# Weights of a mixture of experts on one core: each 1 MB load issued as two of 512 KB

## The chip, the core and the metric

The kernel runs on one core of one Trainium2 chip. The metric is the device time of one execution in microseconds. All arithmetic is float32.

## The reference, cut to what matters

Eight batches (`b`) of 100 tokens with 512 features go through a gated attention-like product with a context of 722 rows per batch, and then through a feed-forward layer with 16 experts, of which each token uses one.

```python
def reference(x, ctx_1024, router_w, w1, b1, w2, b2):
    # xn = layernorm(x)
    x1 = xn @ ctx_1024.T                      # per batch: 100 x 722
    h  = gelu_tanh(x1) * x1
    x  = x + h @ ctx_1024                     # 100 x 512
    # t = layernorm(x), all 800 tokens
    logits = t @ router_w                     # 800 x 16
    assign = argmax(logits)
    g   = sigmoid(logits[assign])
    hh  = gelu(t @ w1[assign] + b1[assign])   # w1: 16 x 512 x 1024
    out = hh @ w2[assign] + b2[assign]        # w2: 16 x 1024 x 512
    return x + g * out
```

Each expert has 2 MB of `w1` and 2 MB of `w2`, so the 16 experts have 64 MB of weights, and all of them are read once.

## The kernel before, in words

The program is written for each engine by hand, with semaphores between them. It has two stages.

**Attention, for b in 0 to 7.** SyncE (SP) loads the transposed context in two parts (`ctxT_a`, `ctxT_b`, line 271), the context itself (lines 266 to 268) and `x` (line 262). Buffers for two batches alternate, so each load for batch b + 2 waits until the products of batch b are done. TensorE computes `x1` (L399) and the second product (L406), VectorE (DVE) the layernorm, the product with the gelu, the residual and the routing: the expert of a token and its rank among that expert's tokens. GpSimd (POOL) scatters each batch's tokens, sorted by expert, into the DRAM tensor `rows` with an indirect DMA (L946).

**Experts.** The sorted tokens are handled in units of 32 tokens of one expert. An expert with more than 32 tokens has several units, and the first expert's first unit and those of the next three (the head) start before the last batch is routed. Per unit j TensorE transposes the tokens (L489), runs `first_layer` (L469, 16 products that the trace shows as x32) and then `second_layer` (L481, 32 products, x64) of unit j - 1. DVE transposes and adds the bias (L804, L810), ScalarE (ACT) does the gelu (L598), DVE the gate and the residual (L828), and POOL scatters the result to the output (L996). Unit lists are computed on the chip: POOL and SP read them from small tables (`colof`, L255) to fetch the units' rows (`load_extra`, L256), and SP fetches the first unit of every expert with `load_first` (L321).

**Weights.** The buffers hold expert 0 (`W1x`, `W2x`) and four slots; slot s takes experts s + 1, s + 5, s + 9 and s + 13. Each of an expert's two matrices is loaded as two halves of 1 MB. `load_half` (L273) issues one half as one DMA from SP (L276): for each of 128 partitions one contiguous piece of 2048 floats, 8 KB, and 16 is added to the half's own semaphore when it has landed. `first_layer` waits for the first half's semaphore before k = 0 and for the second's before k = 2; `second_layer` waits the same way before c = 0 and c = 4. A slot is filled once per round g, so the value waited for is 16 g + 16.

**Order of SP's queue.** What SP issues is carried out in its order, and its waits hold up all that is behind them. During attention, `EARLY` says how many halves are issued after the transposed context of batch b: 0, 0, 1, 1, 1, 2, 4, 3 for b = 0 to 7. Then SP issues two halves (into `W2x`), waits for the scattered rows, issues `load_first`, two halves, two `load_extra`, eight more of `load_first`, the rest of `b2` (L345), and four halves. The halves thus issued fill expert 0's buffers and the four slots. The rest is `next_weights` (L359): when the last unit that needs a slot's `w1` is done (`s_hp`), SP issues the next expert's two halves of `w1`; when it is done with `w2` (`s_y`), the two of `w2`.

```python
def load_half(half, slot, src, signals, h):
    dst = half(slot, h)
    n = dst.shape[1]
    sp.dma_start(dst, src[:, n * h:n * h + n]).then_inc(signals[h], 16)
```

Of the kernel before, what the change touches and what calls it, by code (L numbers as in the profile page):

```python
# [18 lines left out]
E, F = 16, 1024  # L19
# [18 lines left out]
SLOTS = 4  # L38
# [11 lines left out]
EPS = 1e-5  # L50

EARLY = (0, 0, 1, 1, 1, 2, 4, 3)

C_ID, C_NH = 0, P
# [47 lines left out]
def build(nc, x, ctx_main, ctx_rest, ctxT_a, ctxT_b, router, w1, b1, w2, b2, consts, out):  # L103
# [3 lines left out]
    with ExitStack() as stack:  # L107
# [79 lines left out]
        def second_half(slot, h):  # L187
            n = KF // 2
            if slot is None:
                return W2x[:, n * h:n * h + n, :]  # L190
            if slot == SLOTS - 1:
                return late[h][:, :].rearrange("p (k d) -> p k d", k=n)
            return W2[:, slot, n * h:n * h + n, :]
# [56 lines left out]
        def units(eng):  # L250
            return eng.value_load(ends[0:1, E - 1:E], min_val=SLOTS + E, max_val=MAXU)
# [8 lines left out]
        def _(sp):  # L260
# [9 lines left out]
            def load_ctxT(b, part):  # L270
                sp.dma_start(ctxTs[b % 2][part], (ctxT_a, ctxT_b)[part][b]).then_inc(s_ctxT[b % 2][part], 16)

            def load_half(half, slot, src, signals, h):  # L273
                dst = half(slot, h)
                n = dst.shape[1]
                sp.dma_start(dst, src[:, n * h:n * h + n]).then_inc(signals[h], 16)  # L276

            def both(half, slot, w, signals):
                return [(half, slot, w, signals, 0), (half, slot, w, signals, 1)]
# [11 lines left out]
            def load_weights(n):  # L291
                for _ in range(n):
                    load_half(*next(early_weights))
# [11 lines left out]
            for b in range(NB):  # L305
                if b + 2 < NB:
                    for part in range(2):
                        sp.wait_ge(s_x1ps[part], b + 1)
                        load_ctxT(b + 2, part)
                load_weights(EARLY[b])  # L310
                if b + 2 < NB:
# [47 lines left out]
            def next_weights(s, before, first, second):  # L359
                sp.wait_ge(s_hp, before)  # L360
                load_half(first_half, s, first, s_w1[s], 0)
                load_half(first_half, s, first, s_w1[s], 1)
                sp.wait_ge(s_y, before + 1)
                load_half(second_half, s, second, s_w2[s], 0)
                load_half(second_half, s, second, s_w2[s], 1)
# [15 lines left out]
        def _(pe):  # L381
# [5 lines left out]
            def transpose_x2(b):  # L387
                pe.wait_ge(s_x2, b + 1)
                for q in range(Q):
                    last = nc.tensor.transpose(p_t[:, T * q:T * q + T], row[:, b % RB, XW * q:XW * q + DQ],  # L390
                                               ident[0:T, 0:T])
                last.then_inc(s_tps, 1)
# [68 lines left out]
            def first_layer(j, slot, loaded):  # L461
                W, signals = (W1x, s_w1x) if slot is None else (W1[:, slot], s_w1[slot])
                pe.wait_ge(s_cur, j + 1)
                for k in range(KD):
                    if loaded is not None and k % 2 == 0:
                        pe.wait_ge(signals[k // 2], loaded)
                    for q in range(Q):
                        mine = W[:, k, :].rearrange("p (c q i) -> p c q i", c=KF, q=Q)[:, :, q, :]
                        last = nc.tensor.matmul(p_h[U * q:U * q + U, 0:FQ], curT[:, U * k:U * k + U], mine,  # L469
                                                start=(k == 0), stop=(k == KD - 1), tile_position=(0, U * q))  # L470
                last.then_inc(s_hp, 1)

            def second_layer(j, slot, loaded):
                signals = s_w2x if slot is None else s_w2[slot]
                pe.wait_ge(s_yo, j + 2)
                pe.wait_ge(s_act, j + 2)
                for c in range(KF):
                    if c % (KF // 2) == 0:
                        pe.wait_ge(signals[c // (KF // 2)], loaded)
                    for q in range(Q):  # L480
                        last = nc.tensor.matmul(p_y[U * q:U * q + U, 0:DQ], hT[:, U * c:U * c + U],  # L481
                                                second_half(slot, c // (KF // 2))[:, c % (KF // 2), DQ * q:DQ * q + DQ],
                                                start=(c == 0), stop=(c == KF - 1), tile_position=(0, U * q))
                last.then_inc(s_y, 1)

            def transpose_tokens(j):
                pe.wait_ge(s_next, j + 1)
                pe.sem_inc(s_apart_t, 1)
                nc.tensor.transpose(p_blk[:, 0:P], cur, ident).then_inc(s_blk, 1)  # L489
# [1 line left out]
            pe.sem_inc(s_y, 1)  # L491
            transpose_tokens(0)
            transpose_x2(NB - 1)
            first_layer(0, None, 16)
            transpose_tokens(1)
            logits(NB - 1)
            pe.wait_ge(s_b2, 16)
# [3 lines left out]
            ranks(NB - 1)  # L501
            nc.tensor.matmul(p_lg[:, 0:E], ones, hot_sum[:, :], start=True, stop=False)
            nc.tensor.matmul(p_lg[:, 0:E], ones, hot[:, :], start=False, stop=True).then_inc(s_cntps, 1)
            first_layer(1, 0, 16)
            transpose_tokens(2)
            second_layer(0, None, 16)
            pe.wait_ge(s_tab, 16)
            pe.wait_ge(s_pos, NB)
            nc.tensor.matmul(p_rk[0:1, 0:MAXU], unit_f[:, 0:1], ident[0:MAXU, 0:MAXU], start=True, stop=False)
            nc.tensor.matmul(p_rk[0:1, 0:MAXU], unit_f[:, 1:2], packing, start=False, stop=True)  # L510
            nc.tensor.matmul(p_rk[0:1, 64:64 + EXTRA], unit_f[:, 2:3], picked[:, :], start=True, stop=True
                             ).then_inc(s_eofps, 1)
            first_layer(2, 1, 16)
            transpose_tokens(3)
            second_layer(1, 0, 16)
            first_layer(3, 2, 16)
            second_layer(2, 1, 16)
            transpose_tokens(4)
            def end_of(e, least):
                at = slice(e, e + 1) if isinstance(e, int) else bass.ds(e, 1)  # L520
                return pe.value_load(ends[0:1, at], min_val=SLOTS + least + 1, max_val=MAXU)

            def further(first, end, slot, loaded):
                with pe.If(end > first + 1):
                    with pe.Fori(first + 1, end) as j:
                        first_layer(j, slot, None)
                        transpose_tokens(j + 1)
                        second_layer(j - 1, slot, loaded)

            def change(first, slot, loaded, prior, was):
                first_layer(first, slot, loaded)
                transpose_tokens(first + 1)
                second_layer(first - 1, prior, was)

            pe.wait_ge(s_plan, 1)
            change(SLOTS, None, 16, SLOTS - 2, 16)
            end = end_of(0, 0)
            further(SLOTS, end, None, 16)  # L540
            change(end, 0, 16, None, 16)
            with pe.Fori(0, E // SLOTS) as g:
                loaded = pe.snap(16 * g + 16)
                first = end_of(SLOTS * g, 0)
                for s in range(SLOTS - 2):
                    end = end_of(SLOTS * g + (s + 1), s + 1)
                    further(first, end, s, loaded)
                    change(end, s + 1, loaded, s, loaded)
                    first = end
                end = end_of(SLOTS * g + (SLOTS - 1), SLOTS - 1)  # L550
                further(first, end, SLOTS - 2, loaded)

                with pe.If(g < E // SLOTS - 1):
                    first, end = end, end_of(SLOTS * g + SLOTS, SLOTS)
                    change(first, SLOTS - 1, loaded, SLOTS - 2, loaded)
                    further(first, end, SLOTS - 1, loaded)
                    change(end, 0, pe.snap(loaded + 16), SLOTS - 1, loaded)
            second_layer(units(pe) - 1, SLOTS - 2, 16 * (E // SLOTS))

        @block.scalar  # L560
        def _(act):
# [47 lines left out]
        def _(dve):  # L609
# [263 lines left out]
            hidden_bias(3, slice(3, 4))  # L873
            dve.wait_ge(s_eof, 2)
            e4, _, _, after4 = unit_of(SLOTS)
            e5, before5, mine5, after5 = unit_of(SLOTS + 1)
            dve.wait_ge(s_extra[0], 16)
# [184 lines left out]
```

## Time and profile before

| | |
|---|---|
| Median of 3 runs | 298.41 us (295.26 to 300.35) |
| The profiled execution | 296.02 us |
| Its span, first to last instruction | 294.4 us |
| Mean granted TensorE clock | 0.943 |
| PE busy | 243.8 us (83% of the span) |
| DVE, POOL, ACT busy | 120.8, 73.1, 32.4 us |
| SP's queue (q1): packets, MB, share of 16 engines | 18600, 94.48 MB, 86.4% |
| HBM read and written | 95.93 and 5.14 MB, 343 GB/s over the span |
| Half loads into the slots (`W<-in_w`), median from issue to landing | 17.9 us for 1024 KB |

PE is TensorE's matmuls, PEld its weight loads, which overlap them. SPq is the queue of SP's instructions. A DMA's packets are its contiguous pieces, and one small packet per DMA engine that signals completion. A share of 16 engines is the sum of the packets' durations, divided by 16 times the length of the stretch. The chain that ended last is followed back from the last instruction, at each step to what released it. "Issue" stands for time in which an engine waited for nothing that the profile shows.

### The profile page before, as it was taken

The page shows a single profiled execution, that of the slowest core. Times are in us where ns is not written, and L with a number is a line of the kernel's source. Part 1 is how long each engine was busy: PE and PEld are TensorE (multiplying, and loading weights), DVE is VectorE, ACT ScalarE, POOL GpSimd, SP SyncE. Part 2 cuts the span into 40 slices and gives each one's busy share as a digit, 9 for nine tenths or more (in the row PEclk, how much of TensorE's full clock was granted, in tenths as well). Part 3 has the DMA queues.
Part 4 walks back from the last instruction along what each step waited for, and adds up shares of the span by engine and source line. Part 5 has one row for each costly group of instructions (what it writes and reads, how often), then busy time and mean ns, then how long its engine had stood idle before and what let it go on. Part 6 is the DMA issues. An engine that isn't in the chain of part 4 may idle for free.

```text
span 294.4 us, 9782 instructions
## 1 busy us (share of the span) xinstructions
PE 243.8 (83%) x3767; PEld 171.6 (58%) x3768; DVE 120.8 (41%) x424; ACT 32.4 (11%) x76; POOL 73.1 (25%) x97
## 2 busy tenths in 40 slices
PE   0899999999999999995928399777997999679950
PEld 0769587686776845573515167545675666365740
DVE  3035344363443457544413045523544544354520
ACT  0411111110111102010000001101001101001100
POOL 2302032031224314455610111211221221212120
PEclk9999999999999997798877789979999999999995
DMA  6999799999999999799999995899999999999900
GB/s 243 382 383 366 262 337 374 353 365 383 353 414 382 343 378 416 272 323 180 160 325 416 416 380 216 317 340 420 426 419 423 421 424 422 422 421 420 391 28 8
DMA packets 22255, 100.98 MB, mean 343 GB/s; under 512 B 3978, under 2 KB 7950, under 8 KB 13016
## 3 DMA queue, kind: packets, MB, share of 16 engines
q1 hardware_dynamic: 18600, 94.48, 86.4%
q0 software_dynamic: 3488, 5.90, 6.4%
q8 instruction: 17, 0.28, 0.4%
q10 hardware_dynamic: 144, 0.27, 0.2%
q14 instruction: 6, 0.05, 0.0%
HBM read 95.93 MB, written 5.14 MB: 343 GB/s over the span
## 4 chain that ended last, share of the span: by engine, by line
PE 68%; DMA 15%; issue 9%; DVE 2%; SPq 2%; POOL 1%; DVEq 0%; POOLq 0%
PE bank L469 16%; PE bank L481 16%; PE bank L399 15%; PE bank L406 14%; DMA W<-in_w 9%; DMA area<-rows 3%; PE bank L489 2%; DMA rows<-area,pad_at 2%; PE bank L414 2%; PE bank L384 1%; PE bank L390 1%; DMA xs<-in_x 1%; SPq L276 1%; SPq L321 1%; PE bank L422 0%
## 5 line engine op out<-in xcount | busy, mean ns | idle before, releaser
L469 PE MATMUL bank<-W,area 128*32 128x256 f32 x928 | 63.2, 411 | 25.5 <-issue 22.7
L996 POOL DMA_INDIRECT out<-area,out_at x32 | 31.7, 990 | 116.4 <-DVE area L828 107.2
L469 PEld LDWEIGHTS bank<-W,area 128*32 128x32 f32 x928 | 31.0, 117 | 48.0 <-issue 31.7
L481 PE MATMUL bank<-W,area 128*32 128x128 f32 x1600 | 50.6, 279 | 1.8 <-DVE area L828 1.8
L399 PEld LDWEIGHTS bank<-late,area 128*128 128x128 f32 (+1 forms) x384 | 45.1, 195 | 4.7 <-issue 4.6
L481 PEld LDWEIGHTS bank<-W,area 128*32 128x32 f32 x1600 | 43.6, 112 | 5.6 <-DVE area L828 2.2
L406 PE MATMUL bank<-area,late 128*100 128x512 f32 (+1 forms) x96 | 46.8, 601 | 0.0
L399 PE MATMUL bank<-late,area 128*128 128x100 f32 (+1 forms) x384 | 45.5, 281 | 1.3 <-issue 1.3
L804 DVE STREAM_TRANSPOSE area<-bank 128x256 f32<-128x256 f32 x32 | 14.4, 450 | 65.5 <-PE bank L469 64.8
L598 ACT ACTIVATE area<-area 128x256 f32<-128x256 f32 x32 | 13.3, 416 | 153.2 <-PE bank L481 149.2
L946 POOL DMA_INDIRECT rows<-late,pos x8 | 8.6, 1074 | 49.5 <-DVE pos L676 41.4
L406 PEld LDWEIGHTS bank<-area,late 128*100 128x100 f32 (+1 forms) x96 | 13.7, 167 | 10.0 <-issue 10.0
L489 PEld LDWEIGHTS bank<-con,area 128*128 128x128 f32 x33 | 4.7, 143 | 18.5 <-issue 18.5
L632 DVE TENSOR_TENSOR late<-late,bank 128x300 f32<-128x300 f32 x16 | 7.4, 463 | 19.5 <-ACT late L570 19.5
L828 DVE SCALAR_TENSOR_TENSOR area<-bank,area 128x128 f32 (+1 forms) x28 | 9.8, 351 | 10.9 <-PE bank L481 5.6
L489 PE MATMUL bank<-con,area 128*128 128x128 f32 x33 | 11.2, 340 | 3.4 <-DVE area L794 3.3
L810 DVE TENSOR_TENSOR area<-area,b1s 128x256 f32<-128x256 f32 x32 | 13.5, 423 | 1.1 <-DVE area L804 0.2
L570 ACT ACTIVATE late<-bank 128x300 f32<-128x300 f32 x16 | 6.7, 421 | 56.8 <-PE bank L399 56.8
L794 DVE TENSOR_SCALAR area<-area 128x128 f32 (+1 forms) x28 | 10.1, 359 | 6.2 <-DMA area<-rows 4.7
L934 POOL TENSOR_TENSOR late<-ve_t,con 100x4 f32<-100x4 f32 x8 | 8.4, 1053 | 9.6 <-DVE ve_t L618 9.6
L564 ACT COPY late<-bank 128x400 f32<-128x400 f32 x16 | 7.9, 493 | 25.3 <-PE bank L384 21.3
L815 DVE SCALAR_TENSOR_TENSOR area<-xs,area (+1 forms) x28 | 9.8, 351 | 1.3 <-issue 0.4
(114 smaller groups left out, 180.8 us busy)
## 6 DMA issues: line engine op xcount, KB each, us to landing
W<-in_w SPq DMA_DIRECT2D x54, 1024.0 KB, 17.9
area<-in_ctx_main SPq DMA_DIRECT2D x8, 1280.0 KB
area<-in_ctxT_a SPq DMA_DIRECT2D x8, 768.0 KB, 8.9
late<-in_w SPq DMA_DIRECT2D x6, 1024.0 KB, 17.6
area<-in_ctxT_b SPq DMA_DIRECT2D x8, 676.0 KB, 8.0
W1x<-in_w SPq DMA_DIRECT2D x2, 1024.0 KB, 9.9
area<-in_w SPq DMA_DIRECT2D x2, 1024.0 KB, 23.6
xs<-in_x SPq DMA_DIRECT2D x8, 200.0 KB
```

Of the source, the lines that this page charges most:

```text
L399: last = nc.tensor.matmul((p_xa, p_xb)[part][0:n, T * c:T * c + T], ctxTs[b % 2][part][:, k, P * c:P * c + n], xnT[:, k, :], start=(k == 0 ...
L406: last = nc.tensor.matmul(p_att[0:T, :], hidT[0:CW[c], c, :], cxs[b % 2][0:CW[c], c, :], start=(c == 0), stop=(c == SC - 1))
L469: last = nc.tensor.matmul(p_h[U * q:U * q + U, 0:FQ], curT[:, U * k:U * k + U], mine, start=(k == 0), stop=(k == KD - 1), tile_position=(0 ...
L481: last = nc.tensor.matmul(p_y[U * q:U * q + U, 0:DQ], hT[:, U * c:U * c + U], second_half(slot, c // (KF // 2))[:, c % (KF // 2), DQ * q:D ...
L489: nc.tensor.transpose(p_blk[:, 0:P], cur, ident).then_inc(s_blk, 1)
L598: nc.scalar.activation(hT, h_pre, ACT.Gelu).then_inc(s_act, 1)
L794: nc.vector.tensor_scalar(cur, mine[:, 0:DQ], mine[:, DQ + 1:DQ + 2], mine[:, DQ + 2:DQ + 3], ALU.subtract, ALU.mult).then_inc(s_next, 1)
L804: nc.vector.transpose(h_pre, p_h[:, 0:FQ]).then_inc(s_hT, 1)
L810: nc.vector.tensor_tensor(view, view, bias.unsqueeze(3).to_broadcast([P, 2, Q, U]), ALU.add).then_inc(s_hb, 1)
L815: nc.vector.scalar_tensor_tensor(out=mine[:, 0:DQ], in0=bias, scalar=mine[:, DQ:DQ + 1], in1=mine[:, 0:DQ], op0=ALU.mult, op1=ALU.add).the ...
L828: nc.vector.scalar_tensor_tensor(out=y_out[:, at, :].rearrange("p o d -> p (o d)"), in0=p_y[:, 0:DQ], scalar=mine[:, DQ:DQ + 1], in1=mine[ ...
L996: nc.gpsimd.indirect_dma_start(out_q, bass.IndirectOffsetOnAxis(ap=out_at[:, r:r + 1], axis=0), y_out[:, r, :], None, bounds_check=last_ou ...
```

## The change

`load_half` issues two DMAs in place of one. Each has half of the columns: one contiguous piece of 1024 floats, 4 KB, in each of 128 partitions, 512 KB in all. Both add 16 to the half's semaphore, so the half is there at 32, and every wait for a half goes to multiples of 32 (`HALF`). No other operation changes, and buffers, slots and the order of the halves stay.

```diff
+HALF = 32
...
             def load_half(half, slot, src, signals, h):
                 dst = half(slot, h)
                 n = dst.shape[1]
-                sp.dma_start(dst, src[:, n * h:n * h + n]).then_inc(signals[h], 16)
+                for i in range(2):
+                    lo = n // 2 * i
+                    sp.dma_start(dst[:, lo:lo + n // 2], src[:, n * h + lo:n * h + lo + n // 2]
+                                 ).then_inc(signals[h], HALF // 2)
...
-            first_layer(0, None, 16)
+            first_layer(0, None, HALF)
...
             with pe.Fori(0, E // SLOTS) as g:
-                loaded = pe.snap(16 * g + 16)
+                loaded = pe.snap(HALF * g + HALF)
...
-            second_layer(units(pe) - 1, SLOTS - 2, 16 * (E // SLOTS))
+            second_layer(units(pe) - 1, SLOTS - 2, HALF * (E // SLOTS))
```

SP's queue between the attention and the expert stage, before the change; `W<-in_w` is a half of weights into a slot, `area<-in_w` one into `W2x`, `area<-rows` are token rows:

```order
L276 DMA W<-in_w 128x2048 x7
L276 DMA area<-in_w 128x2048 x2
L321 DMA area<-rows 32x4x132 x4
L276 DMA W<-in_w 128x2048 x2
L255 TENSOR_LOAD colof
L255 ISA x2
L256 ISA
L256 DMA area<-rows 128x1x132
```

The same place after it (the lines of code are three or four further down):

```order
L279 DMA W<-in_w 128x1024 x14
L279 DMA area<-in_w 128x1024 x4
L325 DMA area<-rows 32x4x132 x4
L279 DMA W<-in_w 128x1024 x4
L256 TENSOR_LOAD colof
L256 ISA x2
L257 ISA
L257 DMA area<-rows 128x1x132
```

Nothing changed places. Two more DMAs of half the size stand ahead of the read of `colof` and the first `load_extra`.

SP's queue in the loop over experts, one `next_weights`, before:

```order
L371 TENSOR_LOAD ends
L371 ISA x2
L276 ISA
L276 DMA W<-in_w 128x2048
L276 ISA
L276 DMA W<-in_w 128x2048
L363 REGISTER_ALU
L276 DMA W<-in_w 128x2048 x2
```

And after:

```order
L375 ISA x2
L279 ISA
L279 DMA W<-in_w 128x1024
L279 ISA
L279 DMA W<-in_w 128x1024
L279 ISA
L279 DMA W<-in_w 128x1024
L279 ISA
L279 DMA W<-in_w 128x1024
L367 REGISTER_ALU
L279 DMA W<-in_w 128x1024 x4
```

An expert's weights take eight DMAs in place of four, in the same order and behind the same two waits.

## Rows read from the trace of the kernel before

**Rows 1.** The page: 40 slices of 7.36 us, busy tenths and GB/s

```profile
PE   0899999999999999995928399777997999679950
...
DMA  6999799999999999799999995899999999999900
GB/s 243 382 383 366 262 337 374 353 365 383 353 414 382 343 378 416 272 323 180 160 325 416 416 380 216 317 340 420 426 419 423 421 424 422 422 421 420 391 28 8
```

**Rows 2.** Stretches: busy us and count per engine, clock, DMA share, GB/s

```profile
core 0: us, PE busy (x) PEld busy (x) DVE busy (x) ACT busy (x) POOL busy (x), PEclk, DMA share, GB/s
...
36.00:108.00 72.00, 72.00 (x477) 52.60 (x475) 32.15 (x125) 10.73 (x29) 19.29 (x27) 1.00 1.00 362
...
240.00:266.20 26.20, 21.32 (x505) 14.18 (x500) 11.62 (x36) 2.11 (x6) 4.86 (x5) 1.00 1.02 422
266.20:280.00 13.80, 13.55 (x328) 9.47 (x332) 6.87 (x21) 1.25 (x3) 3.71 (x4) 1.00 0.95 396
```

**Rows 3.** Chain that ended last, 239 to 267 us: start, us, what

```profile
239.48 26.63 DMA W<-in_w
...
266.16 1.07 PE bank L469 x16
```

**Rows 4.** Waits of PE and PEld for weights, 240 to 267 us: total, times, longest

```profile
PE bank L469 <- DMA W<-in_w: 2.8, 4, 1.7
...
PEld bank L469 <- DMA W<-in_w: 4.6, 4, 2.2
```

**Rows 5.** DMA by queue, 240 to 266 us: packets, MB, share of 16 engines

```profile
q1 hardware_dynamic: 1463, 10.65, 98.2%
```

**Rows 6.** DMA by queue, 7 to 15 us: the zero fill, pieces of 2112 bytes

```profile
q10 hardware_dynamic: 144, 0.27, 9.0%
```

**Rows 7.** DMA by queue, 136 to 150 us: mostly pieces of 512 and 528 bytes

```profile
q1 hardware_dynamic: 2748, 2.13, 96.2%
```

**Rows 8.** Line 276, duration of an issue: 124.5 to 126, 241 to 256 us

```profile
L276 SPq DMA_DIRECT2D W<-in_w x2: 418/424/429, 124.6 to 125.1; - x2
...
L276 SPq DMA_DIRECT2D W<-in_w x7: 1722/2151/2279, 239.5 to 253.1; - x7
```

**Rows 9.** DMA by queue, 189.9 to 266.2 us

```profile
q1 hardware_dynamic: 4185, 30.45, 97.2%
```

**Rows 10.** Chain that ended last, 117 to 135 us

```profile
117.02 5.53 DMA rows<-area,pad_at
...
125.06 0.43 SPq L276
...
127.09 8.10 DMA area<-rows
```

**Rows 11.** Weight loads of TensorE in order of time, idle before them in brackets

```profile
154.49 0.21 PEld L469 LDWEIGHTS bank<-W,area 128*32 128x32 f32 x8 [5.97 <-issue]
...
167.19 0.20 PEld L469 LDWEIGHTS bank<-W,area 128*32 128x32 f32 x7 [5.08 <-issue]
...
193.06 0.21 PEld L469 LDWEIGHTS bank<-W,area 128*32 128x32 f32 x8 [3.49 <-issue]
```

**Rows 12.** DMA busy tenths, 148 to 168 us and 189 to 193 us, 40 slices each

```profile
DMA  9999989999899999999999999999999999999999
...
DMA  7998997799494391018990466098085097297397
```

**Rows 13.** The end: last matmuls; issue to landing, last two weight transfers

```profile
283.05 1.95 PE L481 MATMUL bank<-W,area 128*32 128x128 f32 x64 [1.60 <-DVE area L828]
...
DMA to landing us min/median/max: 28.1/28.2/28.4
```

**Rows 14.** Line 276 at 96 us (W2x): issues, who waited, issue to landing

```profile
L276 SPq DMA_DIRECT2D area<-in_w x2: 346/400/455, 96.4 to 96.7; - x2
...
  PEld bank L481: 0.9, 1
...
DMA to landing us min/median/max: 22.6/23.6/24.7
```

More of the change, by code:

```diff
@@ L503, in _ @@
             nc.tensor.matmul(p_lg[:, 0:E], ones, hot[:, :], start=False, stop=True).then_inc(s_cntps, 1)
-            first_layer(1, 0, 16)
+            first_layer(1, 0, HALF)
             transpose_tokens(2)
-            second_layer(0, None, 16)
+            second_layer(0, None, HALF)
             pe.wait_ge(s_tab, 16)
@@ L512, in _ @@
                              ).then_inc(s_eofps, 1)
-            first_layer(2, 1, 16)
+            first_layer(2, 1, HALF)
             transpose_tokens(3)
-            second_layer(1, 0, 16)
-            first_layer(3, 2, 16)
-            second_layer(2, 1, 16)
+            second_layer(1, 0, HALF)
+            first_layer(3, 2, HALF)
+            second_layer(2, 1, HALF)
             transpose_tokens(4)
@@ L537, in _ @@
             pe.wait_ge(s_plan, 1)
-            change(SLOTS, None, 16, SLOTS - 2, 16)
+            change(SLOTS, None, HALF, SLOTS - 2, HALF)
             end = end_of(0, 0)
-            further(SLOTS, end, None, 16)
-            change(end, 0, 16, None, 16)
+            further(SLOTS, end, None, HALF)
+            change(end, 0, HALF, None, HALF)
             with pe.Fori(0, E // SLOTS) as g:
-                loaded = pe.snap(16 * g + 16)
+                loaded = pe.snap(HALF * g + HALF)
                 first = end_of(SLOTS * g, 0)
@@ L556, in _ @@
                     further(first, end, SLOTS - 1, loaded)
-                    change(end, 0, pe.snap(loaded + 16), SLOTS - 1, loaded)
-            second_layer(units(pe) - 1, SLOTS - 2, 16 * (E // SLOTS))
+                    change(end, 0, pe.snap(loaded + HALF), SLOTS - 1, loaded)
+            second_layer(units(pe) - 1, SLOTS - 2, HALF * (E // SLOTS))
         @block.scalar
```

## The prediction, made before the kernel was run

> **What bounds the kernel now.** I read the page's slices first. They show two stages: in the first third PE is at 9 tenths with the DMA engines mostly at 7 to 9, and from the slice at 199 us on the DMA engines are at 9 without a break and move 419 to 426 GB/s, while PE drops to 7 and 6 in places [rows 1]. The table of stretches says the same in numbers. From 36 to 108 us PE is busy 72.00 of 72.00 us, so attention is PE's. From 240 to 266 us the DMA share is 1.02 and PE is busy 21.32 of 26.20 us. From 266 to 280 us PE is busy 13.55 of 13.80 us [rows 2]. The chain that ended last joins them: an issue of a half at 239.48 us that takes 26.63 us to land, and PE starts on it at 266.16 us [rows 3]. The reader is to see that the 26.63 us are no latency: ten other halves are ahead of it in the queue. In that stretch PE waits four times on a half of weights, 2.8 us in all, and its weight loads 4.6 us [rows 4]. So the end is set by when the weight stream gets through to that half; behind it PE needs its own 19 us (266.16 us to the end of the matmuls at 285.0 us) [rows 3, 13].
>
> **What a smaller piece costs in the stream.** From 240 to 266 us SP's queue had 98.2% of 16 engines, that is 0.982 x 16 x 26 = 408.5 us, for 10.65 MB, which are 1300 pieces of 8 KB (the other 163 packets signal completion) [rows 5]. That is 314 ns per piece, and 8 x 314 ns = 2.51 us per half and engine. No row has pieces of 4 KB, so I take a straight line through two sizes. The zero fill issued by ACT has pieces of 2112 bytes: 0.27 MB are 128 of them, and 9.0% of 16 x 8 us are 11.5 us, so 90 ns each [rows 6]. The slope is (314 - 90) / (8192 - 2112) = 0.0368 ns per byte, and 4096 bytes come to 163 ns. Two of them take 326 ns where one piece took 314, so 12 ns more, and 8 x 12 = 0.10 us more per half, 4%. Bounds: the low one is nothing (the bytes are the same, and a share of 1.02 leaves no idle time in which a smaller piece could gain). The high one is from the row farthest away: 2748 packets of on average 775 bytes took 0.962 x 16 x 14 = 215.5 us, 78 ns each [rows 7]; less 775 x 0.0368 = 29 ns that is some 50 ns fixed per packet, and with nine more packets per half and engine 0.45 us. I take 0.10 us, since the 2112-byte row is the nearest and came from plain pieces like these, while rows 7 come from a stretch in which two queues pushed small pieces.
>
> The Trainium skill (DMA: Bandwidth & Descriptors, section "iDMA fabric — 4 AXI ports for 8 engines, asymmetric across TPBs") gives 408.7 GB/s for a lone stream of loads with 4 KiB rows. By it a half would take 1.0486 MB / 408.7 GB/s = 2.57 us, where the trace has 422 GB/s; as an estimate that would be 0.08 us more per half and 2.3 us in the first term of the sum below. No 4 KB stream stands in this trace. The same page asks for 1 MiB or more per DMA, since each has some 2 us of fixed cost. The trace disagrees that this is paid in a full queue: at 422 GB/s a half follows the other every 2.5 us.
>
> **How many halves pay it.** From 189.9 us on the queue is never empty until the end: 97.2% of 16 engines to 266.2 us, with 30.45 MB [rows 9]. That is 29.0 halves, one of them under way at 189.9 us, so 28 pass between the restart there and the half that PE waits for at 266.16 us. 28 x 0.10 = 2.8 us, on the path (bounds 0 and 12.6). After that half PE's chain is the longer one: the last two transfers land 28.4 us after their issue at 253.1 us, at 281.5 us, and the matmuls on them start at 283.05 us after a wait for DVE, not for them [rows 8, 13]. Six more halves are 0.6 us later on their own; the room is 1.5 us, and it moves along with the rest. Tail: 0.
>
> **The first stage.** 14 halves are issued before the wait for the scattered rows. They share the engines with the contexts while PE is at 100% [rows 2], so PE's own work hides them; without that cover they would cost 14 x 0.10 = 1.4 us. The last of them, the second half of `W2x`, is issued at 96.7 us and lands 24.7 us later, at 121.4 us, and PE's weight load waited 0.9 us for it [rows 14]. It will be up to 1.4 us late and PE will wait. That wait is covered too: the chain there runs through POOL's scatter (117.02 to 122.55 us), then SP's issues, then `load_extra` from 127.09 to 135.19 us [rows 10], and PE stands idle at its end.
>
> **SP's issues.** One issue takes 0.42 to 0.43 us when the queue has room [rows 8], so a `load_half` costs SP 0.4 us more. In the loop SP has 2.5 us per half and needs 0.85: nothing. It is blocked there anyway, 2.15 us per issue, which shows that only so much fits in the queue. If the limit is in pieces, SP will be 5 halves ahead and not ten, and the stream still doesn't run dry. The one place on the chain is at 125.06 us, where two more issues delay the `load_extra` behind them by 0.9 us. But its transfer lands behind two halves issued just before, the later at 125.06 us, and 8.1 us of queue are ahead of it. What counts there is 2 x 0.10 = 0.2 us plus a little of the issue time. I take 0.3 us (bounds -1.2, if SP is released earlier by a quicker scatter, and 1.4, if the lateness of `W2x` comes through).
>
> **Sum.** 2.8 + 0.3 + 0 = 3.1 us. Against the profiled execution that is 296.0 + 3.1 = 299.1 us; that execution is 2.4 us below the median of the runs, so against the median 298.4 + 3.1 = 301.5 us. PE gets nothing earlier in exchange, since each half still has to be whole before its first matmul.
>
> **Rival 1: other queues get their turn sooner, and the sum comes to 0.** PE's code and POOL's rows travel over the same engines. PE stands still for 5.97 and 5.08 us without a releaser while the engines are full, and for 3.49 us where they are partly idle [rows 11, 12]. The excess of 2.5 and 1.6 us would be a wait behind SP's pieces. With half the bytes per turn half of it goes, 2.0 us, and with the scatter at 117.02 us up to 1.2 us more: -3.2 us against +3.1, so 298.3 us. All of it lies ahead of 189.9 us and moves the stream's restart. For it: the three stalls. Against it: the excess has only one idle case to compare with, and a single piece of 8 KB takes 0.31 us, much less than 2.5. 
>
> **Rival 2: the lengthening is hidden, 298.7 us.** PE waits for halves for only 2.8 and 4.6 us [rows 4]; if PE's own pace set the end, 0.3 us would be left. Against it: the half at 266.12 us is followed by PE at once, so any delay of it passes on in full.
>
> **Rival 3: small pieces cost what rows 7 say, slower by over 2%.** The place is the stream from 189.9 to 266.2 us, the price 0.45 us per half, 28 x 0.45 = 12.6 us, so 311 us. It would exceed 2% (6 us) from 0.21 us per half on, that is 24 ns per extra packet, against the 12 that the line gives. Against it: the line through 2112 bytes.
>
> **How the numbers follow.** 2% is 6.0 us, about what a measurement of this kernel can tell from no change (three runs spread over 5.1 us). Forecast 0.50, rival 1 0.23, rival 2 0.16, rival 3 0.11. The range takes in rivals 1 and 2, with 1.8 us below for the spread of medians of three runs; above the forecast it has room for twice the cost per piece that the line gives (2.8 us) and 1.2 us of that spread: 296.5 to 305.5 us. Slower by over 2% (above 304.4 us): rival 3 and the upper edge of the forecast, 0.15. Faster (below 292.4 us): 0.03, if rival 1's gains were twice as large without the cost. Within 2%: 0.82.
>
> **What would show it.** In the changed profile the stretch from 240 to 266 us should have some 2600 data packets at 163 ns (rows 5), 406 GB/s in place of 422, and PE's last wait for a half should end near 269 us. A rate of 422 would refute the first term, one below 395 would be rival 3. The stalls at 154, 167 and 193 us near 4.7, 4.3 and 3.5 us would be rival 1; unchanged ones refute it. `load_extra` should land at 135.2 to 135.8 us. If PE no longer waits for weights after 240 us, the reading of the bound is wrong.

## The result and the profile after

| | before | after |
|---|---|---|
| Median of 4 runs each | 298.48 us (295.26 to 300.35) | 300.71 us (300.35 to 301.71) |
| Profiled execution, span | 296.02 us, 294.4 us | 301.71 us, 300.1 us |
| Ratio | | 1.0137, 95% interval 1.0082 to 1.0193 |

The change makes the kernel slower by 1.4%; the forecast was slower by 1.0%. (Some runs of nearly every kernel were disturbed and slower: a ratio compares the undisturbed ones, a median is over all runs, and the profiled executions of e6, e9 and e11, which were disturbed, decide nothing below.)

The page's slices of the changed kernel, as in [rows 1]: PE's busy tenths, those of the DMA engines, and GB/s.

```profile
PE   0899999999999995888638599597997989878950
...
DMA  7999899999999999799999995999999999999900
GB/s 250 369 383 366 270 359 374 386 351 366 369 413 376 312 411 402 244 285 183 219 407 334 367 328 168 324 343 403 413 411 408 411 410 410 412 408 411 372 26 7
```

The shape is the old one. In the full stretch at the end the rate is 408 to 413 GB/s, where it was 419 to 426.

The stretches, columns as in [rows 2]:

```profile
36.00:108.00 72.00, 71.91 (x474) 52.35 (x473) 32.10 (x126) 10.73 (x29) 19.30 (x27) 1.00 1.00 366
240.00:266.00 26.00, 21.68 (x504) 15.01 (x508) 11.74 (x37) 2.50 (x6) 5.60 (x6) 1.00 1.03 411
266.00:280.00 14.00, 12.77 (x311) 8.72 (x303) 6.59 (x21) 1.25 (x3) 2.17 (x3) 1.00 1.03 409
280.00:300.00 20.00, 8.75 (x234) 6.69 (x226) 4.29 (x14) 0.83 (x2) 3.89 (x4) 0.84 0.26 102
```

Attention is PE's as before (71.91 of 72.00 us). From 240 to 266 us the DMA engines are full again, at 411 GB/s in place of 422, and they are still full to 280 us.

The chain that ended last. The first fence is one more piece of the kernel before, a second layer that ends at 187.95 + 1.89 = 189.8 us and releases SP; the half that PE waits for last is in [rows 3], and PE is through its first 16 matmuls at 266.16 + 1.07 = 267.2 us.

```profile
187.95 1.89 PE bank L481 x64
```

The same pieces of the changed kernel:

```profile
190.05 1.89 PE bank L485 x64
...
255.28 15.69 DMA W<-in_w
271.01 1.07 PE bank L473 x16
```

The release is at 191.9 us (2.1 later), and the first layer behind the last wait is through at 272.1 us. The stretch between the two takes 80.1 us where it took 77.4: 2.8 us more. The rest of the 5.7 us between the two spans is 0.8 us behind it. The reader can also see what fits into the queue: the transfer lands 15.69 us after its issue, not 26.63. At 411 and 422 GB/s that is 6.4 and 11.2 MB, so the queue's limit is no number of bytes. It is 98 and 86 pieces per engine or 12 and 11 transfers, and this pair can't tell these two apart, since a transfer has eight pieces per engine in both. In e1 and e2 below, where the median from issue to landing from 241 to 256 us was 22.9 and 19.1 us, it comes to 74 and 120 pieces and to 18 and 7 transfers: nearer to a number of pieces, but no fixed one.

PE's waits for weights from 240 to 272 us (total, times, longest), and SP's queue from 240 to 266 us (packets, MB, share of 16 engines), against [rows 4, 5]:

```profile
PE bank L473 <- DMA W<-in_w: 2.5, 2, 1.5
...
PEld bank L473 <- DMA W<-in_w: 3.4, 2, 2.0
```

```profile
q1 hardware_dynamic: 2837, 10.32, 98.9%
```

10.32 MB are 2520 pieces of 4 KB; 98.9% of 16 x 26 us are 411.4 us, so 163 ns per piece.

### The profile page after: what moved, and what is told of

Same layout as the page of the kernel before. It is cut to its first block, busy times and chain, and to the rows that moved or that the text cites. A ratio compares the mean times of both kernels' runs of the same rounds, so it can differ in the third digit from the quotient of the medians.

```text
span 300.1 us, 9894 instructions
## 1 busy us (share of the span) xinstructions
PE 246.5 (82%) x3767; PEld 173.4 (58%) x3768; DVE 120.7 (40%) x424; ACT 32.4 (11%) x76; POOL 72.8 (24%) x97
## 4 chain that ended last, share of the span: by engine, by line
PE 65%; DMA 11%; issue 10%; SPq 8%; DVE 2%; DVEq 1%; POOL 1%; POOLq 0%
PE bank L485 19%; PE bank L473 18%; PE bank L403 11%; PE bank L410 11%; SPq L279 7%; DMA W<-in_w 5%; DMA area<-in_w 5%; PE bank L493 2%; DMA xs<-in_x 1%; PE bank L418 1%; PE bank L388 1%; PE bank L394 1%; SPq L268 0%; DVEq L786 0%; DVE area L832 0%
## 5 line engine op out<-in xcount | busy, mean ns | idle before, releaser
L473 PE MATMUL bank<-W,area 128*32 128x256 f32 x928 | 62.3, 407 | 24.2 <-issue 21.6
L473 PEld LDWEIGHTS bank<-W,area 128*32 128x32 f32 x928 | 31.7, 115 | 45.2 <-issue 30.1
L485 PE MATMUL bank<-W,area 128*32 128x128 f32 x1600 | 52.8, 279 | 2.9 <-DVE area L832 1.8
L485 PEld LDWEIGHTS bank<-W,area 128*32 128x32 f32 x1600 | 44.6, 112 | 8.0 <-issue 2.7
L403 PEld LDWEIGHTS bank<-late,area 128*128 128x128 f32 (+1 forms) x384 | 44.3, 193 | 4.7 <-issue 4.6
L403 PE MATMUL bank<-late,area 128*128 128x100 f32 (+1 forms) x384 | 44.8, 278 | 1.3 <-issue 1.3
L832 DVE SCALAR_TENSOR_TENSOR area<-bank,area 128x128 f32 (+1 forms) x28 | 9.8, 351 | 16.6 <-PE bank L485 12.4
L485 PE MATMUL bank<-area 128*32 128x128 f32 x192 | 8.9, 299 | 6.2 <-DMA area<-in_w 3.7
L493 PE MATMUL bank<-con,area 128*128 128x128 f32 x33 | 11.2, 340 | 0.4 <-DVE area L798 0.3
L485 PEld LDWEIGHTS bank<-area 128*32 128x32 f32 x192 | 6.2, 118 | 8.3 <-issue 6.2
```

The costliest lines, as they stand in the source:

```text
L403: last = nc.tensor.matmul((p_xa, p_xb)[part][0:n, T * c:T * c + T], ctxTs[b % 2][part][:, k, P * c:P * c + n], xnT[:, k, :], start=(k == 0 ...
L832: nc.vector.scalar_tensor_tensor(out=y_out[:, at, :].rearrange("p o d -> p (o d)"), in0=p_y[:, 0:DQ], scalar=mine[:, DQ:DQ + 1], in1=mine[ ...
```

## The experiments

The theories: A, the fixed time of each piece lengthens the stream that bounds the last third; B, it is the number of transfers; C, shorter turns on the engines let other queues through sooner, which wins something back. In each run the full stretch is read at 240 to 262 us, and the length of the stream from the end of the sixteenth second layer to the end of the first layer behind the last wait, as above. The kernel before ran beside all of them, on the same chip. The edits of e1, e3 and e8 are shown against the changed kernel, the others against the kernel before.

**e1: two transfers, pieces of 8 KB.**

```diff
+                for i in range(2):
+                    sp.dma_start(dst[i::2], src[i::2, n * h:n * h + n]).then_inc(signals[h], HALF // 2)
```

> Each half as two transfers of 512 KB, but in pieces of 8 KB: one takes the even partitions, one the odd. Theory A (the cost sits in the piece): as before the change, ratio 1.000 within 0.004, and 422 GB/s in the full stretch near the end with 314 ns per piece. Theory B (the cost sits in the number of transfers, their completions and issues): as the change, ratio 1.010 to 1.015 and about 411 GB/s. Theory C (shorter turns let PE's code and POOL's rows through sooner): faster than before by 1 to 3 us, ratio 0.990 to 0.997.

Ratio 1.0046 (1.0003 to 1.0089), medians 296.5 against 294.96 us. Stretches and SP's queue in its profile, two windows and one:

```profile
206.00:240.00 34.00, 31.11 (x758) 22.15 (x754) 17.32 (x54) 2.94 (x8) 7.76 (x8) 1.00 1.01 422
240.00:262.00 22.00, 17.67 (x392) 11.33 (x386) 8.87 (x28) 1.67 (x4) 3.88 (x4) 0.92 1.01 422
...
q1 hardware_dynamic: 1378, 9.02, 98.2%
```

422 GB/s with two transfers per half: B falls for the rate, and the ratio too is below the 1.010 to 1.015 that B asked for. C's gain did not come either.

**e2: one transfer, pieces of 4 KB.** The source has a gap of 64 floats behind every 1024.

```diff
+                dst = dst.rearrange("p (i m) d -> p i (m d)", i=2)
+                sp.dma_start(dst, src[:, 2 * h:2 * h + 2, 0:PIECE]).then_inc(signals[h], 16)
...
+    def apart(a):
+        return np.pad(a.reshape(E, P, 4, PIECE), ((0, 0), (0, 0), (0, 0), (0, 64)))
```

> Each half as one transfer of 1 MB, but in pieces of 4 KB: in DRAM each piece of 4 KB is followed by 256 unused bytes, so that two don't join. Theory A (the piece): as the change, ratio 1.010 to 1.015, about 411 GB/s near the end, 163 ns or a little less per piece. Theory B (the number of transfers): as before, ratio 1.000, 422 GB/s. Theory C (shorter turns help, pieces cost): slower than the change itself by 1 to 3 us.

Ratio 1.0045 (0.9996 to 1.0094), medians 297.8 against 294.96 us. The same views:

```profile
206.00:240.00 34.00, 30.95 (x764) 22.14 (x759) 17.68 (x55) 3.16 (x8) 7.77 (x8) 1.00 1.03 411
240.00:262.00 22.00, 16.48 (x388) 10.97 (x388) 9.36 (x29) 1.84 (x5) 3.89 (x4) 1.00 1.03 411
...
q1 hardware_dynamic: 2267, 8.76, 99.1%
```

411 GB/s with one transfer per half, the rate of the change. The piece alone sets the rate: A. The whole time did not rise to the 1.010 to 1.015 that A expected, though its stream took 79.2 us, 1.8 more than in the kernel before. So neither the pieces (e2) nor the two transfers (e1) alone cost in the whole time what the change cost on the same chip (e0 below).

**e3: four transfers, pieces of 2 KB**, with 16 from each and waits for multiples of 64.

```diff
-HALF = 32
+HALF = 64
...
+                for i in range(4):
+                    sp.dma_start(to, at).then_inc(signals[h], HALF // 4)
```

> Each half as four transfers of 256 KB in pieces of 2 KB, all on the half's semaphore. Theory A with a fixed time per piece: three times the cost of the change, since 3 more pieces per 8 KB where the change has 1 more: 0.3 us per half, some 395 GB/s near the end, and 28 halves give +8 us, ratio 1.025 to 1.035. Theory B (number of transfers): also about three times, so this run alone does not tell them apart. A cost of the first stage that is not in the stream would not triple: then 1.012 to 1.02.

Ratio 1.0238 (1.0138 to 1.0338), medians 304.89 against 294.96 us.

```profile
206.00:240.00 34.00, 28.65 (x698) 20.16 (x690) 15.80 (x50) 2.92 (x7) 7.76 (x8) 0.99 1.05 389
240.00:262.00 22.00, 18.95 (x388) 12.81 (x388) 9.01 (x28) 1.67 (x4) 3.88 (x4) 0.86 1.05 389
...
q1 hardware_dynamic: 4574, 8.33, 102.5%
```

389 GB/s, lower than the 395 expected, and a ratio just under the 1.025 to 1.035 expected. Its stream took 84.5 us: 7.1 more, 2.5 times the change's 2.8.

**e0: the change again.**

> The change itself again, unaltered, beside the other three on the same chip. Ratio 1.008 to 1.019 as measured; 411 GB/s near the end. If its span this time is 2 to 3 us above that of the kernel before where the profiled executions differed by 5.7 us, then half of that difference was scatter between executions.

Ratio 1.0229 (1.0171 to 1.0288), medians 301.95 against 294.96 us, above the 1.008 to 1.019 expected, and the interval barely meets the first measurement's (1.0082 to 1.0193). Its profiled execution was its fastest (span 295.8 us, 1.4 above the profile before): release at 189.1 us, stream 79.6 us, 410 GB/s. So the 2.1 us that the first profile showed ahead of the release come and go between executions; the stream's part does not.

**e4 and e5: only the halves of the loop, only those before it.** `FIRST` and `STEP` are 16 and 32 in e4, 32 and 16 in e5. The expectations speak of 24 halves before the loop; the traces have 20 (20 transfers of 1024 KB in e4, 40 of 512 KB in e5), and 44 in it.

```diff
+            def load_half(half, slot, src, signals, h, parts=FIRST // 16):
...
+                m = n // parts
+                for i in range(parts):
+                    sp.dma_start(dst[:, m * i:m * i + m], src[:, n * h + m * i:n * h + m * i + m]
+                                 ).then_inc(signals[h], 16)
...
+                loaded = pe.snap(STEP * g + FIRST)
```

> Only the halves of the loop over experts (those issued behind s_hp and s_y) come as two transfers of 4 KB pieces; the 24 halves issued before it stay one transfer of 8 KB pieces. From the release at about 190 us to PE's last wait for a half: 2.2 to 2.8 us longer than in the kernel before, as in the change. If the stream is all of the cost, ratio 1.007 to 1.010. If the rest of the change's cost (it measured 2.3% on one chip, 6 us) arises ahead of the loop, this run stays well below the change.

> Only the 24 halves issued before the loop come as two transfers of 4 KB pieces; those of the loop stay as before. Stretch from 190 us on as in the kernel before (77.4 us from the sixteenth second layer to the first layer behind the last wait), 422 GB/s. By the prediction's terms the front costs 0.3 us: ratio 1.001. If the front holds what the stream doesn't explain: ratio 1.005 to 1.013 (1.5 to 4 us), lost between 119 and 155 us, where PE waits for the halves of W2x.

e4: ratio 1.0219 (1.0148 to 1.0291), medians 299.27 against 294.28 us. e5: 1.0123 (1.007 to 1.0175), 296.41 against 294.28 us. The stretch from 240 to 262 us, first e4, then e5:

```profile
240.00:262.00 22.00, 16.95 (x398) 11.08 (x389) 9.02 (x28) 1.67 (x4) 4.75 (x5) 1.00 1.03 411
```

```profile
240.00:262.00 22.00, 17.37 (x420) 11.60 (x412) 9.91 (x32) 2.08 (x5) 3.88 (x4) 1.00 1.02 422
```

411 GB/s with the late halves split, 422 with only the early ones, and streams of 80.1 and 76.6 us: the stream's cost sits in the halves of the loop. But e4's ratio is above the 1.007 to 1.010 expected if the stream were all of the cost, although nothing ahead of the loop is changed in it. e5's front was late in its profile. TensorE's matmuls on `W2x`, in order of time, with the idle time before them:

```profile
121.30 1.94 PE L485 MATMUL bank<-area 128*32 128x128 f32 x32 [1.76 <-DMA area<-in_w]
125.35 1.93 PE L485 MATMUL bank<-area 128*32 128x128 f32 x32 [2.12 <-DMA area<-in_w]
```

The second 32 start at 125.35 us, behind a wait for the half; in the kernel before the half landed at 121.4 us [rows 14]. Not all of that lateness comes from the early halves. TensorE gets to the third batch's first product at 37.21 us, 1.54 us later than in the kernel before (35.67 us), and SP issues the first half of weights only at 42.94 us. Half of the 3.2 us by which this profile's release is late (193.0 against 189.8 us) was there before any half was issued.

**e6: the change a third time.**

> The change itself, beside the two partial ones on the same chip. If the two parts add up, its ratio less 1 is the sum of theirs, within 0.006. Ratio between 1.008 and 1.029, by the two intervals measured so far.

Ratio 1.0249 (1.0172 to 1.0327), medians 301.75 against 294.28 us. The two parts' ratios add up to 1.034, which is 0.009 more than that where 0.006 was allowed, with intervals of 0.005 to 0.008 to each side. And e4 alone (1.0219) is not told apart from the whole change.

**e7: the other direction, pieces of 16 KB in the loop.**

```diff
-                load_half(first_half, s, first, s_w1[s], 0)
-                load_half(first_half, s, first, s_w1[s], 1)
+                sp.dma_start(W1[:, s], first).then_inc(s_w1[s][0], 16)
```

> The kernel before, but in the loop over experts each matrix comes as one transfer of 2 MB in pieces of 16 KB (except w2 into the last slot, whose two halves lie apart). The three rates so far (422, 410 and 389 GB/s near the end, for 8, 4 and 2 KB) fit a fixed time of 8.8 ns per piece. Theory A: 16 KB pieces give some 427 GB/s near the end, and the stretch from the release at 190 us to the last gate gets 1.0 us shorter less up to 1 us, since PE now waits for both halves of w1 at once: ratio 0.997 to 1.001. If the fixed time is no property of the piece, 422 GB/s and 1.000 to 1.004.

Ratio 1.0053 (0.9993 to 1.0112), medians 295.55 against 295.66 us: no difference.

```profile
206.00:240.00 34.00, 30.96 (x748) 21.72 (x740) 17.07 (x54) 3.33 (x8) 7.60 (x8) 1.00 1.00 426
240.00:262.00 22.00, 17.93 (x452) 12.90 (x448) 10.68 (x34) 1.75 (x5) 4.03 (x5) 1.00 1.02 430
...
q1 hardware_dynamic: 776, 9.19, 98.3%
```

430 and 426 GB/s, and a stream of 76.2 us, 1.2 us shorter. The rate went as A said; the time shows no gain that these runs can tell.

**e8, e9, e10: W2x ahead in the queue**, in the change, in the kernel before, and together with e7's pieces.

```diff
-EARLY = (0, 0, 1, 1, 1, 2, 4, 3)
+EARLY = (0, 0, 1, 1, 1, 2, 4, 1)
...
-                                 + second_weights(0) + second_weights(1) + both(second_half, None, w2[0], s_w2x)
+                                 + second_weights(0) + both(second_half, None, w2[0], s_w2x) + second_weights(1)
...
             sp.wait_ge(s_att, NB - 1)
-            load_weights(2)
+            load_weights(4)
```

> The change, but the four transfers into W2x are issued ahead of those of the second matrix of slot 1, as soon as the buffer is free, so that they are some 5 us earlier in the queue. If what the front costs beyond the forecast comes through PE's wait for W2x (seen at 118 to 130 us), that wait goes and only the stream's 2.2 to 2.8 us are left: ratio 1.006 to 1.011. If the front's cost has another place, the ratio stays at that of the change, 1.014 to 1.025.

> The same reordering in the kernel before. There W2x made PE wait 0.5 us and the chain did not run through it: ratio 0.995 to 1.001. If it gains as much as it does in the change, W2x was no cost of the change.

> Both together on the kernel before: W2x ahead, and whole matrices in pieces of 16 KB in the loop. If their effects add up: 0.993 to 1.001, the fastest of all so far.

e8: ratio 1.0199 (1.0128 to 1.0269), 300.22 us. e9: 1.0144 (1.0068 to 1.0219), 298.5 us. e10: 1.0016 (0.9939 to 1.0093), 297.78 us. The kernel before: 295.66 us. By e9 the reordering itself loses, against the 0.995 to 1.001 expected, but e10 has it too and does not: e7's and e9's ratios would add up to 1.020. What the reordering costs is not settled. Two of PE's waits in e8, 110 to 300 us:

```profile
PE bank L473 <- DMA W<-in_w: 7.2, 7, 1.6
PE bank L493 <- DVE area L798: 7.0, 1, 7.0
```

PE no longer waits for `W2x`, but for 7.0 us on the tokens that DVE makes from the rows of `load_extra`, and in all it gains nothing. The change costs 1.7 us between the medians of e9 and e8, which is of the size of the stream's part, but each of them has six runs that spread over 5 to 7 us.

**e11: e5 once more.**

> The run with only the 24 early halves as two transfers of 4 KB pieces once more, since its ratio (1.007 to 1.0175) and its one profile (PE waits for W2x until 125.4 us, 3.9 us later than in the kernel before) rest on few executions. If the front's cost is real: ratio 1.004 or more again, and PE's wait for the second half of W2x ends after 122 us. If it was scatter between executions: ratio within 0.997 to 1.004, and the wait ends near 121 us as in two of the profiles of the change.

Ratio 0.9982 (0.9917 to 1.0047), medians 298.61 against 297.41 us. It does not repeat e5's 1.0123, but only three of its twelve runs count in the ratio, and over all twelve it is 1.2 us slower. In its profile, one of the three that decide nothing, PE's wait for the second half of `W2x` ends at 126.66 us, past the expectation's 122. So the front's cost stays unsettled.

The length of the stream, by the size of the pieces in the loop, over the other eleven profiles:

| pieces in the loop | runs | release at, us | release to last gate, us | GB/s at 240 to 262 us |
|---|---|---|---|---|
| 16 KB | e7, e10 | 187.9, 189.4 | 76.2, 76.2 | 430, 427 |
| 8 KB | before, e1, e5 | 189.8, 186.4, 193.0 | 77.4, 78.2, 76.6 | 423, 422, 422 |
| 4 KB | after, e0, e2, e4, e8 | 191.9, 189.1, 189.6, 186.7, 191.9 | 80.1, 79.6, 79.2, 80.1, 80.0 | 410, 410, 411, 411, 411 |
| 2 KB | e3 | 189.8 | 84.5 | 389 |

In e1 PE does not wait for a half at the gate, so its 78.2 us are PE's own pace there. Behind the gate every profile takes 27.1 to 28.0 us. The stream thus goes by the size of the pieces, and nearly all other difference between the profiles, 6.6 us, lies ahead of the release. The release comes at 190.5 us in the mean of the five with two transfers per early half (after, e0, e1, e5, e8) and at 188.7 us in the five with one, a difference of 1.8 us that is smaller than the spread within either group (6.6 and 3.1 us).

The means are 77.4 us for 8 KB and 79.8 us for 4 KB. 8 KB take 16 x 8192 / 422 = 310.6 ns of an engine in one piece, 319.3 ns in two (410.5 GB/s) and 337.0 ns in four: 8.7 and 8.8 ns for each piece more.

## Why the prediction was right

**The bound** was read rightly. PE waits for a half until 271.01 us and starts on it as it lands. That is 2 us behind the 269 us asked for, by as much as the release was late; in e0 it was 267.65 us. e4 puts the stream's cost into the loop's halves, and rival 2 (hidden) falls with the stream's 2.4 us.

**The cost of a piece.** 163 ns were forecast from the line through 2112 bytes and 163 were measured. Yet the rate fell by 2.7% and not by 4%, to 411 and not to 406 GB/s: the sum of the packets' durations went from 102 to 103% of the engines' time, so part of the longer sum overlaps. The term was 0.10 us per half, the rate makes it 1.0486 MB x (1/410.5 - 1/422.5) = 0.07 us, and the measured stream makes it 2.4 / 28 = 0.09 us. The Trainium skill's 408.7 GB/s (DMA: Bandwidth & Descriptors, "iDMA fabric — 4 AXI ports for 8 engines, asymmetric across TPBs") agrees with this case's 410 to 411 GB/s better than the line did. Rival 3 (0.45 us per half) falls: even pieces of 2 KB cost 7.1 / 28 = 0.25 us. Its outcome, over 2%, was nevertheless the ratio of e0 and e6, with intervals that reach below 2%, and not by its mechanism.

**The number of halves and the tail.** 28 x 0.10 = 2.8 us was the forecast, 2.8 us the first pair of profiles, 2.4 us the mean of all. The tail was 0.8 us longer in the first profile (28.0 us from the gate to the end, before 27.2) and 27.1 in e0 and e2: nothing.

**SP's issues.** The queue reached six halves ahead in place of ten, where the forecast had five, and the stream didn't run dry. Before the expert stage SP is held up too, in the chain of the changed kernel:

```profile
97.86 4.68 SPq L279
...
104.90 15.40 DMA area<-in_w
...
121.17 1.06 PE bank L485 x11
```

One issue of `W2x` takes 4.68 us, and the last one leaves at 104.90 us, where it left at 96.7 us. It still lands at 120.3 us, where it landed at 121.4 us, and PE starts on it at 121.17 us. So the issue that came 8 us later cost nothing here.

**The front** was forecast at 0.3 us, with 1.4 us as the upper bound. This is the step that the runs do not bear out well. The first measurement fits it: 2.8 + 0.3 us stand against 2.2 us between the medians. On the two later chips (e0 and e6) the change cost 7.0 and 7.5 us between the medians, and the stream explains 2.4 of them, so up to some 5 us are not in the stream.

One price in the front was too small. The forecast gave two more transfers ahead of `load_extra` 0.2 us and a little. The scatter and the landing of `load_extra` in e0, e1 and e2, against [rows 10]:

```profile
116.43 5.24 DMA rows<-area,pad_at
...
126.62 9.23 DMA area<-rows
```

```profile
116.35 5.35 DMA rows<-area,pad_at
...
127.49 8.79 DMA area<-rows
```

```profile
117.38 5.38 DMA rows<-area,pad_at
...
127.33 7.03 DMA area<-rows
```

From the end of the one to the landing of the other it takes 14.2 and 14.6 us in e0 and e1, with two transfers per half, and 11.6 us in e2, which has small pieces but one transfer. In the kernel before it is 12.6 us. e8 (two) has 14.6 us, e4 and e10 (one, there) have 12.1 and 12.4. So what costs here is the number of transfers, some 2 us: SP's issues between the two took 0.9 to 1.0 us for two transfers and 1.9 to 2.4 us for four, and the rest is the transfer itself, 8.8 to 9.2 us in place of 7.0 to 8.1. That these 2 us reach the end is not shown: the releases in the table differ by 1.8 us in the mean, but e1 has the 2 us and the earliest release of all.

Where the rest sits is open. e5 put 0.7 to 1.75% into the early halves, and e11 did not repeat it. e1 and e2, which have one half of the change each, show 1.5 and 2.8 us over the median before. Against the front speaks e4, whose front is the old one: 5.0 us between the medians, 2.7 us in the stream. Moving `W2x` ahead (e8) did not bring anything back. One rival was not tested, TensorE's clock. In the kernel before, PE's first layer at 115.06 us took 3.64 us at a granted clock of 0.50, its lower level (1.2 GHz), where in the changed one, at 1.00 (2.4 GHz), it took 1.93 us. On the chip of e4 to e6 the mean granted clock of the runs in the ratios was 0.958 for the kernel before, 0.941 in e4 and 0.937 in e6; on that of e0 it was 0.949 and 0.945. Whether the lower clock made those runs longer or came with longer waits, no run shows.

**Rival 1** (stalls of PE's code get shorter) went by the stalls. In the changed kernel, then in e0, weight loads with their idle time:

```profile
156.59 0.94 PEld L473 LDWEIGHTS bank<-W,area 128*32 128x32 f32 x20 [4.76 <-issue]
...
168.63 0.20 PEld L473 LDWEIGHTS bank<-W,area 128*32 128x32 f32 x7 [4.54 <-issue]
...
195.60 0.20 PEld L473 LDWEIGHTS bank<-W,area 128*32 128x32 f32 x8 [3.94 <-issue]
```

```profile
154.18 0.21 PEld L473 LDWEIGHTS bank<-W,area 128*32 128x32 f32 x8 [5.36 <-issue]
...
166.89 0.20 PEld L473 LDWEIGHTS bank<-W,area 128*32 128x32 f32 x7 [5.08 <-issue]
...
192.86 0.20 PEld L473 LDWEIGHTS bank<-W,area 128*32 128x32 f32 x8 [4.03 <-issue]
```

Against 5.97, 5.08 and 3.49 us [rows 11] the first two are 1.2 and 0.5 us shorter in one profile and 0.6 and 0.0 us in the other, the third is longer in both; 4.7, 4.3 and 3.5 had been asked for. In sum they are 1.3 us shorter in the one and unchanged (14.5 us) in the other. All of PE's idle time without a releaser from 126 to 196 us was 15.8 us before, 17.6 and 17.5 us in the two profiles of the change, so what one stall lost others gained. e1, which halves the turns and leaves the pieces, had 14.0 us but wasn't faster. The gain of 3.2 us is refuted. The rule of whole packets per turn (the Trainium skill, DMA: Bandwidth & Descriptors, "Queues, rings and completion order") is not shown wrong by this; if turns are as it says, halving them gained nothing in the whole time here.

**The total.** 301.5 us was forecast and 300.71 measured. The forecast's ratio is 1.010, the three measurements' are 1.014, 1.023 and 1.025, so it was low rather than high. The stream's term is right by its mechanism. That the whole time came out so near is in part luck: the first measurement was the smallest of three, and no term of the sum covers what made the other two larger.

## What to carry to other kernels

Where the DMA queue is full and on the path, count the pieces that a transfer is made of, not the transfers: on this chip each contiguous piece cost 8.8 ns of an engine beyond its bytes, 3% at 4 KB against 8 KB. Two transfers that signal one semaphore bring nothing for the waiting engine, which still needs both, and they lengthened the way of a small transfer issued behind them by some 2 us. With pieces half as long the queue reached 15.7 us ahead in place of 26.6, which cost nothing while no engine ran dry. Two profiles of the same changed kernel were 4.3 us apart (spans 300.1 and 295.8 us) with streams 0.5 us apart: a difference of 1% is better read in the stage where it should arise than in the whole time.

## What had not been expected

Packet durations and rate do not move alike: two pieces of 4 KB took 327 ns in the records where one of 8 KB took 314, while the rate fell by only 2.7%. With pieces of 2 KB SP's queue alone had 102.5% of 16 engines. An issue over every second partition (e1) took SP 0.60 us, where the plain one took 0.42 us. And the change's median against the kernel before was +2.2, +7.0 and +7.5 us on three chips, though the intervals of the ratios just meet.
